# Five value products, two weight roundings and one weight transfer moved by a step at the start of a fused attention stage

## What is computed

```
x = x + xattn0(layernorm(x), ctx);  x = x + ffn0(layernorm(x))
q = rmsnorm(layernorm(x) @ Wq.T, 32 heads);  k, v = rmsnorm(ctx @ Wk.T), ctx @ Wv.T, 8 heads of 128
x = x + softmax(q k.T / sqrt(128) + mask) v  @ Wo.T        # over the 128 rows of the same sequence
x = x + down(silu(gate(layernorm(x))) * up(layernorm(x)))  # int weights, dequantized
```

## Time and profile before

| | |
|---|---|
| median of 3 runs | 850.12 us (850.08 to 850.28) |
| the profiled execution, whole | 850.66 us |
| its span, first to last instruction | 848.9 us |
| TensorE busy | 820.1 us, 97% of the span |
| VectorE / ScalarE / GpSimd busy | 564.5 / 534.3 / 549.2 us |
| TensorE clock granted | full in all 40 slices |
| attention calls, about | 194 to 650 us |

### The profile page before, as it was taken

How to read it: one execution, slowest core, us unless ns; L and a number is a source line. 1 busy time by engine, 2 the same in 40 slices (tenths; PEclk the granted TensorE clock), 3 DMA queues, 4 the chain that set the end, 5 groups by cost and what they waited for, 6 DMA issues and landing times.

```text
span 848.9 us, 13289 instructions
## 1 busy us (share of the span) xinstructions
PE 820.1 (97%) x3932; PEld 671.7 (79%) x3932; DVE 564.5 (66%) x990; ACT 534.3 (63%) x1769; POOL 549.2 (65%) x554
## 2 busy tenths in 40 slices
PE   6899999999989999999999999999999999999995
PEld 5687888788778888888888888888887777777773
DVE  5605762532656666666666666666568899999996
ACT  4543461144677777777777777777677477667763
POOL 3332562321577777777777777777676268999995
PEclk9999999999999999999999999999999999999999
DMA  8510567204566666766667766667754023344302
GB/s 275 178 51 26 142 169 191 83 1 112 160 191 195 187 176 183 201 187 187 185 188 223 217 191 191 187 193 189 235 150 149 0 78 146 149 149 149 143 6 100
DMA packets 96037, 129.76 MB, mean 153 GB/s; under 512 B 25757, under 2 KB 68637, under 8 KB 95966
## 3 DMA queue, kind: packets, MB, share of 16 engines
q1 hardware_dynamic: 95966, 128.92, 51.0%
HBM read 89.82 MB, written 39.06 MB: 152 GB/s over the span
## 4 chain that ended last, share of the span: by engine, by line
PE 79%; DVE 7%; DMA 6%; ACT 2%; issue 2%; POOL 2%; SPq 1%; POOLq 0%; DVEq 0%; ACTq 0%
PE pair L1605 18%; PE pair L1607 18%; PE pair L1606 18%; PE pair L1763 8%; PE pair L1764 8%; PE pair L1857 5%; DMA land<-block_bounce 2%; DMA block_bounce<-tb 2%; SPq L577 1%; PE pair L1625 1%; DVE kv L1474 1%; DMA resid<-in_x_dram 1%; PE pair L1664 1%; PE pair L1715 1%; DVE st L1202 1%
## 5 line engine op out<-in xcount | busy, mean ns | idle before, releaser
L1605 PE MATMUL pair<-split,xnT_hi 128*128 128x512 f32 x288 | 113.3, 394 | 0.3 <-issue 0.3
L1607 PE MATMUL pair<-split,xnT_lo 128*128 128x512 f32 x288 | 112.1, 389 | 0.0
L1606 PE MATMUL pair<-split,xnT_hi 128*128 128x512 f32 x288 | 112.1, 389 | 0.0
L964 ACT ACTIVATE headT<-land,wqk 128x512 f32<-128x512 f32 x62 | 44.9, 725 | 89.9 <-DMA land<-block_bounce 65.6
L1605 PE MATMUL pair<-split,aoT_hi 128*128 128x512 f32 x244 | 95.7, 392 | 0.4 <-DVE resid L1408 0.4
L1607 PE MATMUL pair<-split,aoT_lo 128*128 128x512 f32 x244 | 95.2, 390 | 0.0
L1606 PE MATMUL pair<-split,aoT_hi 128*128 128x512 f32 x244 | 94.9, 389 | 0.0
L985 ACT ACTIVATE prob<-pair,nmax 128x128 f32<-128x128 f32 x244 | 86.0, 362 | 13.6 <-DVE nmax L1386 13.4
L1763 PE MATMUL pair<-xnT_hi,split 128*128 128x512 f32 x224 | 90.8, 405 | 2.0 <-DVE kv L1529 1.2
L739 POOL TENSOR_TENSOR prob<-prob,rinv 128x512 f32<-128x512 f32 x61 | 63.6, 1043 | 39.0 <-DVE rinv L1356 39.0
L1764 PE MATMUL pair<-xnT_lo,split 128*128 128x512 f32 x224 | 87.6, 391 | 0.0
(11 more groups left out here) (183 smaller groups left out, 2154.6 us busy)
## 6 DMA issues: line engine op xcount, KB each, us to landing
block_bounce<-tb SPq DMA_DIRECT2D x244, 128.0 KB, 2.3
land<-block_bounce SPq DMA_DIRECT2D x61, 512.0 KB, 3.4
raw<-in_wqo_dram SPq DMA_DIRECT2D x62, 256.0 KB, 3.0
kv<-in_ffn_w_dram SPq DMA_DIRECT2D x14, 768.0 KB, 4.3
kv<-in_ffn_z_dram SPq DMA_DIRECT2D x14, 768.0 KB, 5.6
kv<-key_bounce SPq DMA_DIRECT2D x32, 128.0 KB, 2.9
key_bounce<-tb SPq DMA_DIRECT2D x44, 64.0 KB, 2.0
resid<-in_x_dram SPq DMA_DIRECT2D x2, 1024.0 KB, 9.4
```

Source lines behind the costliest of these rows:

```text
L1605: pe.matmul(dst, l_hi, r_hi, start=first, stop=False)
L1606: pe.matmul(dst, l_hi, r_lo, start=False, stop=False)
L1607: return pe.matmul(dst, l_lo, r_hi, start=False, stop=last)
```

## The change

PE makes v(11) to v(15) each one call later (v(14), in call -2, at the head of that call; the others behind the query product of theirs), so that call -6 has none and call -1 has v(15). ACT's copies move with them; in call -1 the copy of v(15) and behind it the rounding of chunks 8 and 9 stand at the call's end, behind the exponentials of item 3, where the rounding stood behind the squares. POOL's remainder of chunk 8 moves to the end of its call -1. SP's transfer of chunk 10 moves behind `bounce_write(6)`. Nothing is added or left out.

```diff
-        VALUES_AT = {-6: (11,), -5: (12,), -4: (13,), -3: (14,), -2: (15,)}
+        VALUES_AT = {-5: (11,), -4: (12,), -3: (13,), -2: (14,), -1: (15,)}
...
             def step(j):
                 if 0 <= j + LEAD - 1 < STEPS:
                     bounce_read(j + LEAD - 1)
+                if j + LEAD < STEPS:
+                    bounce_write(j + LEAD)
                 if j == 0:
                     group_chunk(10)
-                if j + LEAD < STEPS:
-                    bounce_write(j + LEAD)
...
-                if j == -1 and p is None:
-                    weight_lo(POOL_EARLY, None)
...
+                if j == -1:
+                    weight_lo(POOL_EARLY, None)
...
-                for n in EARLY_CHUNKS.get(j, ()) if p is None else ():
-                    weight_hi(n, None)
-                for m in VALUES_AT.get(j, ()) if p is None else ():
-                    copy_values(m)
+                if j != -1:
+                    for n in EARLY_CHUNKS.get(j, ()):
+                        weight_hi(n, None)
+                    for m in VALUES_AT.get(j, ()):
+                        copy_values(m)
...
                     done.then_inc(s_ex, 1)
+                if j == -1:
+                    copy_values(2 * T - 1)
+                    for n in EARLY_CHUNKS[j]:
+                        weight_hi(n, None)
...
-                for m in VALUES_AT.get(j, ()) if p is None and j < -2 else ():
+                for m in VALUES_AT.get(j, ()) if j != -2 else ():
                     values(m)
```

## The result

The changed kernel takes **855.84 us** (median of five, 854.00 to 856.14) against 850.28 (850.08 to 851.52) for the kernel before: ratio 1.0061, 95% interval 1.0050 to 1.0073. It is slower by 5.6 us. The prediction said slower by 2.6 and put the upper end of its range at 854.0: the sign came out, and so did the chain of waits up to attend(2); the size was off by a factor of two, for the greater part because TensorE's clock fell, which the prediction did not have.

A forecast was written before the change was run, and what follows sets the result against it. TensorE was taken to bound the kernel, its stalls at the attention stage's begin counting one for one. Chunk 10's rounding at 241.23 instead of 238.59 gave 850.12 + 2.64 = 852.76, or 852.8 us; range 851.9 to 854.0.

The forecast's parts named there:

- the chain of waits up to attend(2): Stage's begin: late chunk 10 is rounded 2.64 us later and, 4.89 us behind, attend(2) comes at 246.12 instead of 243.48.
- TensorE bounds the body, and what it is late by at 257 us stays: Attention body, 257 to 570 us: TensorE is always busy, so lateness at its begin reaches the end one for one.
- Value products: Calls -6 to -1: products one call later bring the exponentials of item 3 at 229.92 instead of 232.44, 2.52 us earlier.
- Copy and rounding behind the exponentials eat the lead: Call -1: 1.53 us of ScalarE work and 1.0 waiting for chunk 9's remainder leave item 3's reciprocal at 233.96, before 233.95.
- slower still: Stage's begin: chunk 8's and 9's remainders hinder each other, or write traffic slows chunk 10; 1 to 2 us more, chance 0.09.
- Chunk 10's landing: Transfer behind bounce_write(6): issued at 238.43 instead of 234.46, taking 2.8 us instead of 4.11, landing at 241.23.
- From there the body runs as before: From attend(2) on: no further stall or change in the body, so the kernel ends 2.64 us later.
- the 6.1 us of stalls: Stage's begin: TensorE's stalls grow from 3.48 by 2.64 us, about 2 ahead of attend(1), 1 of s(5), the rest of attend(2).
- the lead of the first part: Stage's begin: the 2.52 us gained by moving the value products, forecast to be eaten whole on the way to DVE.

The follow-up runs named there:

- filled kernel: The changed kernel with 10, 5 and 8 unread matmuls of 512 columns inside TensorE's three stalls at the attention stage's begin: 854.16 us, ratio 1.0030 to before.
- Values alone: The kernel before with only the five value products and their copies one call later, roundings, remainder and chunk 10's transfer unmoved: 847.24 us, 847.06 when run again.

## Why the prediction was wrong

By its own steps:

- **TensorE bounds the body, and what it is late by at 257 us stays.** Right: +4.42 us at attend(3), +4.36 at the end's last stall.
- **Value products.** Right: the exponentials of item 3 came within 0.02 us of the forecast, and moving only these is worth over 3 us.
- **Copy and rounding behind the exponentials eat the lead.** Right in kind, undersized by 0.30 us. The remainder of chunk 9 was taken at 0.95, from a row in which it stood beside another GpSimd operation; here it stood beside the remainder of chunk 8 and took 1.34. The prediction weighed the Trainium skill's exclusion ("SBUF — State Buffer", "Who interferes with whom") against that row and went by the row. The trace agrees with the rule: GpSimd's operation ended at 232.81 and VectorE's at 233.36, 0.55 later; apart from it, it took 0.69. The row itself was misread. It is not a milder price: in the kernel before, VectorE's remainder, started at 232.14, had another and shorter GpSimd operation beside it first,

```profile
232.09 0.46 POOL L758 TENSOR_TENSOR vcur_lo<-kv,vcur_hi 128x128 fp32r<-128x128 f32 x1 [0.44 <-ACT vcur_hi L971]
```

which ended at 232.55; VectorE's ended at 233.09, 0.54 later. Reckoned in this way, from the end of chunk 8's remainder (233.78 in the forecast), it would have been 234.3 instead of 233.96, which is what came (234.27 for the reciprocal on the clock of before), and not the 234.7 that the prediction names for the rule. Of the rival "slower still" this is the first half, at 0.3 us.
- **Chunk 10's landing** was taken at 2.8 and took 3.16, +0.36. In the four profiles with this order on the queue it took 2.77, 3.16, 3.24 and 4.09, so 2.8 was a possible value at the lower end. Together 2.64 + 0.30 + 0.36 = 3.30, against 3.29 measured up to attend(2). The chain is accounted for; this far the forecast would have been inside its range (850.12 + 3.3 = 853.4).
- **"From there the body runs as before": the step that failed.** It priced a stall of TensorE at its length. TensorE stood idle for 6.9 us between 231 and 246, its clock was at half from 243.4 to 250.2, and 2.12 us more were lost from attend(2) to attend(3). (The 0.84 at the end are no part of the change.) No rival of the prediction has this term; even "slower still" ends at 855. The page's line of the clock, full in all slices before, was taken as given and not as something that stalls can change. The filled kernel shows the error: the same chain without the idle time runs 1.7 us shorter.

The Trainium skill ("TensorE: Matmul & The Clock Gate", section "Part 1: The HAM clock gate (the "warmup" mystery)") says that the throttled clock is the default and that activity releases it; it would have been a rival of its own, and the prediction named none. The filled kernel agrees with it: with matmuls in the stalls the clock stayed full from attend(0) to attend(3). With this rival the 6.1 us of stalls should have carried a price for a stretch of matmuls at half clock; in these rows a matmul of 512 columns then takes 0.427 instead of 0.227 us from start to start.

The forecast said that the lead of the first part is lost again; it did not say that the other two parts need not have been made. It found that the roundings lose 2.5 us on the path, but took the moves as belonging together. Values alone shows that they don't.

## What to carry to other kernels

When a product is moved, leave what hangs on it at the first gap in which it can run, and look at the queue of the transfers last: a load that the next step waits for must not stand behind a write that waits for the end of this one. Price a stall of TensorE of two to three microseconds above its length, whether it stands alone or close to others, unless another wait behind it hides the loss; if it can't be removed, filling it with unread matmuls gets part of the time back (1.7 us here). And take the profile of several executions before you call a clock full: the one at hand had a fuller clock than each of 53 later runs of the same kernel.

## What was not expected of the hardware

- A stall of 2.84 us was followed by 3.4 us at half clock in one profile and by full clock in the other, with the same instructions ahead of it; one of 2.25 us was followed by 3.4 us at half clock in one kernel, and one of 2.26 by none in another. A fall lasted 3.4 or 6.8 us and added 1.6 to 2.5 us to TensorE's work.
- Transfers of 256 KB with the same neighbours on the queue landed after 2.77 to 4.09 us.
- VectorE's subtraction of two SBUF tiles, 0.69 us alone, took 1.34 when a GpSimd one had started 0.48 us before it. Beside a long and beside a short GpSimd operation it ended 0.54 to 0.55 us after that operation's end; the wait shows as a longer duration and not as idle time.
